# Attention block with a group norm ahead of it, one core: where the group norm's small products stand in TensorE's and VectorE's orders

## The reference

```python
g = gn(x)                         # group norm, 32 groups of 24 channels, eps 1e-5
qkv = g @ qkv_w.T + qkv_b         # 2304 outputs
q += g @ la_q.T @ lb_q.T ;  v += g @ la_v.T @ lb_v.T
# 12 heads of 64; per image and head
attn = (q * 64**-0.5) @ k.T + rel_h(q) + rel_w(q)    # 196 x 196
out = softmax(attn) @ v
y = x + out @ proj_w.T + proj_b
```

## Time and profile before

| what | value |
|---|---|
| median of three runs | 3322.74 us |
| the profiled execution's own time | 3322.35 us |
| its span in the trace | 3320.5 us |
| TensorE (PE) busy | 3203.9 us, 96% |
| VectorE (DVE) busy | 2750.2 us, 83% |
| ScalarE (ACT) busy | 2124.7 us, 64% |
| 16 DMA engines, the busiest queue | 59.3% |
| mean granted TensorE clock | 0.981 of full speed |

### The profile page before, as it was taken

The page is one execution under the profiler, slowest core; times in us unless marked ns, Lnnn a source line. Parts: engine busy times, 40 slices in busy tenths (PEclk is TensorE's granted clock), DMA queues, the critical chain, the costliest instruction groups (busy, mean ns, idle before and its releaser), DMA issues.

```text
span 3320.5 us, 78578 instructions
## 1 busy us (share of the span) xinstructions
PE 3203.9 (96%) x31280; PEld 1999.0 (60%) x31280; DVE 2750.2 (83%) x5490; ACT 2124.7 (64%) x5491; POOL 35.2 (1%) x65
## 2 busy tenths in 40 slices
PE   7489999999999999999999999999999999999997
PEld 4255666666666666666666666666666666666664
DVE  7688888888888888888888888888888888888874
ACT  3366666666666666666666666666666666666663
POOL 0100000000000000000000000000000000000000
PEclk6799999999999999999999999999999999999999
DMA  3157766567766666776666777666677666677654
GB/s 130 39 107 136 140 126 120 124 132 137 143 139 118 121 124 128 149 140 123 120 127 130 139 143 134 120 120 128 128 148 140 123 117 127 130 141 143 124 103 101
DMA packets 1267533, 420.09 MB, mean 127 GB/s; under 512 B 1092824, under 2 KB 1247448, under 8 KB 1267168
## 3 DMA queue, kind: packets, MB, share of 16 engines
q1 hardware_dynamic: 1251334, 377.69, 59.3%
q10 hardware_dynamic: 15834, 37.37, 3.8%
HBM read 86.60 MB, written 38.54 MB: 38 GB/s over the span
## 4 chain that ended last, share of the span: by engine, by line
PE 64%; DVE 22%; ACT 7%; issue 3%; DMA 1%; SPq 0%; POOL 0%; DVEq 0%; ACTq 0%; POOLq 0%
PE ring L554 34%; PE ring L621 14%; PE score L597 6%; DVE split L801 5%; ACT prob L686 5%; PE o_ps L611 5%; DVE sums L821 3%; DVE row_max L779 3%; PE ring L576 3%; PE ring L627 2%; DVE split L793 1%; DVE x_sb L845 1%; DVE k_lo L746 1%; DVE rel_sb L772 1%; DVE v_split L754 1%
## 5 line engine op out<-in xcount | busy, mean ns | idle before, releaser
L554 PE MATMUL ring<-xn,w_hi 128*128 128x392 f16 x6912 | 1713.0, 329 | 12.9 <-DMA xn<-xs 12.5
L554 PE MATMUL ring<-xn,w_lo 128*128 128x392 f16 x3456 | 1133.6, 328 | 0.0
L686 ACT ACTIVATE prob<-score,neg_max,exp_scale 98x196 f32<-98x196 f32 x1536 | 769.9, 510 | 306.4 <-DVE neg_max L783 303.2
L554 PEld LDWEIGHTS ring<-xn,w_hi 128*128 128x128 f16 x6912 | 643.1, 96 | 482.6 <-DMA xn<-xs 11.9
L801 DVE SCALAR_TENSOR_TENSOR split<-prob,row_inv,split 98x196 f16<-98x196 f32 x1536 | 545.6, 418 | 8.9
L779 DVE TENSOR_REDUCE row_max<-score 98x4 f32<-98x784 f32 x384 | 372.2, 969 | 165.4 <-PE score L597 165.3
L554 PEld LDWEIGHTS ring<-xn,w_lo 128*128 128x128 f16 x3456 | 331.8, 96 | 244.2 <-issue 2.9
L621 PE MATMUL ring<-o_hi,w_hi 128*128 128x392 f16 x1152 | 380.6, 330 | 1.4 <-DVE o_lo L810 1.4
L621 PE MATMUL ring<-o_hi,w_lo 128*128 128x392 f16 x1152 | 379.7, 330 | 0.0
L621 PE MATMUL ring<-o_lo,w_hi 128*128 128x392 f16 x1152 | 379.7, 330 | 0.0
L696 ACT ACTIVATE split<-prob,row_inv 98x196 f16<-98x196 f32 x768 | 310.2, 454 | 72.3 <-DVE row_inv L787 71.5
(11 more groups left out here) (114 smaller groups left out, 4494.8 us busy)
## 6 DMA issues: line engine op xcount, KB each, us to landing
y_sb<-in_x SPq DMA_DIRECT2D x192, 196.0 KB
out<-y_sb SPq DMA_DIRECT2D x192, 196.0 KB
x_sb<-in_x ACTq DMA_DIRECT2D x31, 1176.0 KB
rel_q<-rel_sb SPq DMA_DIRECT2D x128, 122.5 KB, 2.3
stage<-in_L_conv_qkv_w SPq DMA_DIRECT2D x3, 2304.0 KB, 15.0
turned<-split SPq DMA_TRANSPOSE x384, 4.2
rel_q<-rel_sb SPq DMA_DIRECT2D x128, 24.5 KB, 2.1
v_tok<-v_split SPq DMA_TRANSPOSE x192, 3.7
```

The source lines that it names most:

```text
L554: last = T.matmul(ring[:, bank, 0:NT], w[:, c, 128 * j:128 * j + 128], xn[:, par, xx, :, c, 0:HALF], start=(c == 0 and part == 0), stop=(c ...
L686: last = A.activation(prob[:, head, half, :], score[0:HALF, head, TOK * half:TOK * half + TOK], ACT.Exp, bias=neg_max[:, k % 2, i:i + 1], ...
```

## The change

One entry of TensorE's order is moved a projection ahead, another a projection back, and VectorE's steps on them go likewise.

```diff
 PE_ORDER = (
-    each("S", 0, 0) + each("P", 1, 10) + each("Z", 2, 5) + each("V", 0, 0) + each("K", 0, 1)
-    + each("S", 0, 1) + each("P", 1, 11) + each("G", -1, 1) + each("V", 0, 1) + each("G", -1, 2) + each("Y", 1, 0)
+    each("S", 0, 0) + each("P", 1, 10) + each("Z", 2, 5) + each("V", 0, 0) + each("G", -1, 1) + each("K", 0, 1)
+    + each("S", 0, 1) + each("P", 1, 11) + each("V", 0, 1) + each("G", -1, 2) + each("Y", 1, 0)
...
-    + each("S", 0, 8) + each("P", 0, 6) + each("G", -2, 0) + each("Q", -1, 4, 5)
+    + each("S", 0, 8) + each("P", 0, 6) + each("Q", -1, 4) + each("G", -2, 0) + each("Q", -1, 5)
...
 DVE_ORDER = (
-    each("S", 0, 0) + each("D", -1, 1) + soft(0) + each("Z", 2, 4) + each("V", 0, 0) + each("Z", 2, 5)
-    + each("S", 0, 1) + each("G", -1, 1) + each("K", 0, 1) + each("P", 1, 11) + each("E", -1, 0) + soft(1)
+    each("S", 0, 0) + each("D", -1, 1) + soft(0) + each("Z", 2, 4) + each("V", 0, 0) + each("Z", 2, 5) + each("G", -1, 1)
+    + each("S", 0, 1) + each("E", -1, 0) + each("K", 0, 1) + each("P", 1, 11) + soft(1)
...
-    + each("S", 0, 8) + each("Q", -1, 3) + each("G", -2, 0) + soft(8) + each("Q", -1, 4) + each("B", -2, 0)
+    + each("S", 0, 8) + each("Q", -1, 3) + soft(8) + each("G", -2, 0) + each("Q", -1, 4) + each("B", -2, 0)
```

## The result

The changed kernel takes 3346.94 us (median of four runs, 3343.61 to 3347.31), the kernel before beside it 3322.97 (3322.59 to 3324.18). The ratio is 1.0068, 95% interval 1.0055 to 1.0080: 24 us slower. Forecast were 3340.5, with a range of 3334 to 3347. So the direction and most of the size were right, and 6 us are missing from the sum: the measured median lies at the very edge of the range.

A forecast was written before the change was run, and what follows sets the result against it. TensorE's work plus its stops was taken as the bound. Part 1's loss of 27.3 less gains of 7.0 at G 0 and 2.5 in the ramp gave +17.8 us, so 3340.5, range 3334 to 3347.

The forecast's parts named there:

- main case: Whole kernel: G 1 waits for D 1, G 0 and the ramp gain; 3340.5 us, own range 3336 to 3344, chance 77%.
- rival (c): VectorE at S 10: its 0.17 of waiting is missing; every 0.1 adds 3 us, up to 3350; chance 12%.
- Part 1, G 1: TensorE's G 1 ahead of K 1 waits for D 1; G 2 comes 0.92 us later each round, 27.3 us lost.
- The 0.8 that stops ahead of P 10 were to spare: Four rounds where TensorE already stopped longer ahead of P 10: the loss is together about 0.8 us less.
- Part 2, G 0: TensorE's G 0 behind Q 4: the wait for A 1, 0.24 a round, goes; 7.0 us gained.
- forecast 2.5 - 1.4 = 1.1: Ahead of round 2: 2.5 us gained in the ramp, about 1.4 lost in round 1, still settling.
- The ramp: Ahead of the second pair's G 0: Q 5, R and the first S 0 come sooner; 2.5 us gained, bounds 0 and 2.7.
- (a): D 1 at G 1's new place: the sum of squares is in time; -12.4 us, so 3310; chance 5%.
- (b): G 1's wait for D 1: VectorE's lag shrinks by some 0.6 us; no change, 3322; chance 4%.
- (d): TensorE's clock: each round's 1.2 us stop brings the low clock; 51 us more, 3391; chance 2%.

The follow-up runs named there:

- half of D 1: The changed kernel with VectorE's D 1 summing the squares of one tile in place of two; 3323.73 us.
- G 1 alone: Against the kernel before, only G 1 is moved (with VectorE's G 1 and E), G 0 in its old place; 3354.20 us, ratio 1.0091.
- G 0 alone: Against the kernel before, only G 0 is moved, the entries of G 1 and E as before; 3318.16 us, ratio 0.9982.

## Why the prediction was right, and the step that was short

**The bound.** TensorE in order, a gain or loss counted once a round: held in every experiment.

**The number.** The direction and the mechanism of the main case were right; that the measured time still lies inside 3334 to 3347 is luck. It is outside the main case's own 3336 to 3344, and the top of the range was there for rival (c), which did not happen.

**Part 1, G 1.** The mechanism is right as written, the sum is some 2.5 us short. The three times from S 0 are off by 0.05 at most, the wait for D 1 is there 29 times in the stretch shown, shorter where P 10 had already stopped TensorE. D 1's end sets it (half of D 1), and a place 3 us later ends it (G 1 behind K 1). That D 1's end doesn't move when TensorE is slowed was argued from VectorE's wait at S 10; the changed kernel shows it, 6.03 in the median of the rounds before and after. From the S 0 of round 2 to that of round 31, G 1 alone is 2876.0 us long and the kernel before 2847.5: 28.5 for 29 rounds, 0.98 each, against 0.92 each and 25.9 in all forecast. Distances taken from other contexts are some of it: G 1 to the projection behind it is 0.18 (0.15 assumed), a projection to the step of another shape 3.09 (3.08). The 0.8 that stops ahead of P 10 were to spare is not seen in the total; their number differs from run to run. (The prediction counts D 1's end at 6.03 to 6.05 in 24 of rounds 2 to 30; the trace has 6.02 to 6.05 in 25 and 5.5 to 5.8 in four, which changes nothing.)

**Part 2, G 0.** This is the step that failed: the term 29 × 0.24 = 7.0 us counts the whole gain at G 0 and puts the wait that it makes at R 0 at nothing. In rounds 2 to 30 of the profiled executions G 0 alone gains 1.5 us in place of 7.0. Its gain on TensorE, 0.24 a round, was there and even 0.05 more: G 0 to Q 5 is 0.14 where G 0 to Q 4 was 0.19. But I followed the copy of the means, moved behind T 8, only to S 10, where 0.17 of VectorE's wait was to be left, and never asked who else waits for what it pushes. R 0 does: it needs VectorE's Q 5 read. The timelines of the kernel before have VectorE's Q 5 and TensorE's R 0 so:

```profile
1016.14 0.62 DVE L749 SCALAR_TENSOR_TENSOR xs<-ring,bias,xs 128x392 f16<-128x392 f32 x1
```
```profile
1017.11 0.16 PE L561 MATMUL ring<-w_hi 128*128 128x2 f16 x1
```

Q 5's low part ends at 1016.76 and R 0 starts at 1017.11, 0.35 later; a matmul that waited for Q 5, D 1 or A 1 starts 0.14 to 0.15 after its end, so 0.20 was free. TensorE came 0.29 earlier and VectorE 0.13 later, 0.42 in all, and R 0 stands 0.21 a round. The timelines in the changed kernel, VectorE and then TensorE:

```profile
1120.06 0.62 DVE L749 SCALAR_TENSOR_TENSOR xs<-ring,bias,xs 128x392 f16<-128x392 f32 x1
...
1126.47 0.98 DVE L779 TENSOR_REDUCE row_max<-score 98x4 f32<-98x784 f32 x1 [0.34 <-PE score L597]
```
```profile
1112.95 0.31 PE L639 MATMUL ring<-sums,gmean 98*98 98x64 f32 x2
...
1116.98 0.70 PE L611 MATMUL o_ps<-turned,v_tok 98*64 98x196 f16 x12
...
1120.82 0.16 PE L561 MATMUL ring<-w_hi 128*128 128x2 f16 x1
```

Q 5 ends at 1120.68, R 0 starts at 1120.82, 0.14 later. At S 10 VectorE waits 0.34 and not the 0.17 that I had, because R 0's stop gives 0.21 of it back. 29 × 0.21 = 6.0 us, and moving B 0 out of Q 5's way took just these back. That 17.8 + 6.0 comes to 23.8 for the measured 24.0 is in part because other errors cancel. In the profiled executions the changed kernel loses 26.0 us over rounds 2 to 30, where the terms for them come to 18.9 (29 × 0.92 - 0.8 - 7.0). The 7.1 between are, to 0.1, R 0's 5.9 and Part 1's 2.5, less the 1.4 by which the gain at G 0 was larger. A round in which nothing else stops TensorE takes 99.10 us against 98.85 forecast. Outside of these rounds 1.5 us are gained ahead of round 2 (forecast 2.5 - 1.4 = 1.1) and 0.2 at the end.

**The ramp.** The stop of 2.49 ahead of the second pair's G 0 is gone, and the first S 0 starts at 158.3 in place of 160.5: 2.2 of the 2.5. How exact that is can't be said: in the profiled executions of the other runs it starts at 155.5 to 157.8 where G 0 is moved and at 160.9 to 161.4 where it is not.

**The rivals.** (a) fell: from round 1 on, no round had D 1 in time. (b) fell: the wait didn't shrink over the rounds. (c), VectorE behind at S 10, did not come; what came was its neighbour, VectorE behind at Q 5, which I had not listed. (d) fell: the granted clock between 300 and 3250 us is 1.00 in the changed kernel, with a stop of 1.1 us in each round.

## What to carry to other kernels

Ahead of moving a small product on a full engine, set its new time of arrival beside the end of what it reads; here 1.2 us too early cost more than both waits that the change removed. A wait of some tenths can be covered by a step that is already there: the consumer one large step later (G 2 behind Y 0), or the producer ahead of a neighbour with slack (A 1 ahead of V 4). And when an engine gets earlier by some tenths, or the other's step later, list every consumer of every pushed step with its slack, not only the place where the two engines meet.

## What the runs showed of the hardware that was not expected

The small product G 2, with weights of 64 rows, runs beside the scores behind it, which use 64 rows too: the first matmul of S 2 starts 0.01 us behind G 2 and the next 0.13, where between two projections it takes 0.29 to 0.31 from G 2 to the one behind it. The Trainium skill, page TensorEngine Tiling (Array Packing), section Key Properties, says that tiles work independently, with loads and matmuls of different tiles in parallel, and the interleaved rows above agree; which rows of the array each matmul used, the timeline doesn't say. The same section says that a switch of mode drains TensorE, and the trace agrees: G 1, whose two passes stream one column each, costs 0.21 between K 1 and S 1, and 0.06 behind P 11, whose weights have its shape.

The wait of a weight load can be far longer in the records than its price: 12.2 us of idle for L561 stood for 6.0 us of time, and with A 1 moved early the same line shows 5.7 us, while R 0 starts 3.00 behind K 5's first matmul as before. In the records the load stands idle while matmuls of the projection ahead still run.
